# Three PSUM banks in turn for h, gate and up, three for the mixer, and new orders of the steps

## The reference

```python
zxbcdt = u @ W_in                        # 256 -> 512 (z) + 768 (x, B, C) + 8 (dt)
xBC = silu(causal_conv4(xBC) + conv_b)   # four taps along the tokens
dt = softplus(dt + dt_bias);  A = -exp(A_log)
y, _ = ssd(x * dt, A * dt, B, C, 32)     # a state-space scan, 8 heads of 64, state 128
y = (y + x * D) * silu(z)
y = y * rsqrt(mean(y**2) + EPS) * norm_scale
x1 = layernorm(u + y @ W_out)
```

```python
gate, up = x1 @ dequant(Wg).T, x1 @ dequant(Wu).T      # 256 -> 2048 each
out = layernorm(x1 + (gelu(gate) * up) @ dequant(Wd).T) # 2048 -> 256
```

## Time and profile before

| | |
|---|---|
| median of 3 runs | 956.86 us (954.81 to 960.31) |
| profiled execution | 955.87 us, span 954.1 us |
| PE busy | 853.1 us (89%), 5476 products |
| DVE busy | 709.3 us (74%) |
| ACT busy | 546.9 us (57%) |
| GpSimd busy | 70.0 us (7%) |
| mean granted clock of TensorE | 0.962 of full |

### The profile page before, as it was taken

How to read it: one execution, slowest core, us unless ns; L and a number is a source line. 1 busy time by engine, 2 the same in 40 slices (tenths; PEclk the granted TensorE clock), 3 DMA queues, 4 the chain that set the end, 5 groups by cost and what they waited for, 6 DMA issues and landing times.

```text
span 954.1 us, 16326 instructions
## 1 busy us (share of the span) xinstructions
PE 853.1 (89%) x5476; PEld 743.2 (78%) x5476; DVE 709.3 (74%) x1600; ACT 546.9 (57%) x1002; POOL 70.0 (7%) x105
## 2 busy tenths in 40 slices
...
GB/s 135 137 27 62 42 117 106 23 34 73 140 13 23 66 145 55 22 66 113 87 22 44 88 127 6 22 66 146 54 22 67 123 79 13 56 102 1 1 34 12
DMA packets 37578, 61.32 MB, mean 64 GB/s; under 512 B 3264, under 2 KB 25888, under 8 KB 37536
## 3 DMA queue, kind: packets, MB, share of 16 engines
...
q10 hardware_dynamic: 432, 0.03, 0.0%
...
## 4 chain that ended last, share of the span: by engine, by line
PE 61%; DVE 14%; DMA 8%; issue 8%; ACT 5%; POOL 3%; SPq 1%; DVEq 0%; POOLq 0%; ACTq 0%
DMA dec<-spread 5%; PE gate_bank L535 5%; PE mixer L535 5%; PE up_bank L535 5%; PE up_bank L537 5%; PE up_bank L536 4%; PE gate_bank L537 4%; PE gate_bank L536 4%; PE down L535 4%; PE mixer L537 4%; PE down L536 4%; PE down L537 4%; PE mixer L536 4%; PE mixer L602 3%; ACT dec L764 2%
## 5 line engine op out<-in xcount | busy, mean ns | idle before, releaser
L535 PE MATMUL down<-wd_hi,in_hi 128*128 128x256 f32 x512 | 144.4, 282 | 1.0 <-DVE in_lo L1062 1.0
L536 PE MATMUL down<-wd_lo,in_hi 128*128 128x256 f32 x512 | 143.1, 279 | 0.0
L537 PE MATMUL down<-wd_hi,in_lo 128*128 128x256 f32 x512 | 142.8, 279 | 0.0
L535 PE MATMUL gate_bank<-hT_hi,wg_hi 128*128 128x512 f32 (+1 forms) x288 | 113.8, 395 | 23.6 <-ACT act_sb L797 23.6
L931 DVE SCALAR_TENSOR_TENSOR xbc<-mixer,chan,xbc 128x510 f32<-128x510 f32 (+1 forms) x162 | 110.9, 684 | 26.6 <-ACT xbc L732 25.4
L1062 DVE TENSOR_TENSOR in_lo<-act_sb,in_hi 128x512 fp32r<-128x512 f32 (+1 forms) x144 | 90.0, 625 | 51.7 <-ACT in_hi L783 51.0
L783 ACT ACTIVATE in_hi<-act_sb 128x512 fp32r<-128x512 f32 (+1 forms) x144 | 82.7, 574 | 64.3 <-PE down L537 53.0
L1076 DVE SCALAR_TENSOR_TENSOR act_sb<-up_bank,act_sb 128x512 f32<-128x512 f32 (+1 forms) x144 | 90.3, 627 | 37.9 <-PE up_bank L537 19.3
L535 PE MATMUL up_bank<-hT_hi,wu_hi 128*128 128x512 f32 (+1 forms) x288 | 107.7, 374 | 5.6 <-DVE act_sb L1076 5.6
L797 ACT ACTIVATE act_sb<-gate_bank 128x512 f32<-128x512 f32 (+1 forms) x144 | 78.7, 547 | 50.7 <-PE gate_bank L537 50.1
L537 PE MATMUL up_bank<-hT_hi,wu_lo 128*128 128x512 f32 (+1 forms) x288 | 107.3, 373 | 0.0
...
## 6 DMA issues: line engine op xcount, KB each, us to landing
...
```

The costliest lines, as they stand in the source:

```text
L535: nc.tensor.matmul(dst, lh, rh, start=first, stop=False, skip_group_check=True)
L536: nc.tensor.matmul(dst, lh, rl, start=False, stop=False, skip_group_check=True)
L537: return nc.tensor.matmul(dst, ll, rh, start=False, stop=last, skip_group_check=True)
```

## The change

Of the eight banks, three (`ffn0` to `ffn2`) now serve h, gate and up in turn, three the mixer, and two down as before. Gate of unit n goes to a bank that up of unit n-2 had, so it waits for inter of unit n-2; up of unit n goes to the bank that gate of unit n-1 had, so it waits for that gelu. The order of the mixer's steps is new in the first run and in full groups (z products between the x products; A one slot earlier; H and L of a tile together), the last group keeps its lists. Chunks 0 to 12 are now done in the first run and 13 to 23 in the second, one behind each unit, all with take-off and lower; the subtraction on DVE is gone. `dt`'s links, and SP's places for `spread`, `load_uT` and `keep_h`, are new too.

```diff
+MIXER_BANKS = 3
-    "full": ["dt", "x4", "x5", "x0", "z0", "x1", "CB0", "CB1", "z1", "x2", "z2", "A", "x3", "z3", "XT0", "Y0", "XT1",
-             "Y1", "Yoff0", "XT2", "S0", "op0", "Y2", "XT3", "S1", "op1", "Y3", "Yoff1", "S2", "op2", "S3", "op3"],
+    "full": ["dt", "x4", "z0", "x5", "x0", "z1", "x1", "z2", "x2", "x3", "A", "z3", "CB0", "XT0", "CB1", "Y0",
+             "XT1", "S0", "op0", "Y1", "Yoff0", "XT2", "Y2", "XT3", "S1", "Y3", "Yoff1", "op1", "S2", "op2",
+             "S3", "op3"],
...
-    "full": [["x5"], ["x0", "z0"], ["x1", "CB0", "CB1", "z1"], ["x2", "z2"], ["A", "x3", "z3"], ["H0"],
-             ["L0", "XT0", "X0", "W0"], ["Y0", "H1"], ["L1", "XT1", "X1", "W1"], ["Y1", "g0", "H2"],
-             ["L2", "XT2", "X2", "S0", "W2"], ["op0", "g1", "Y2", "H3"], ["L3", "XT3", "X3", "S1", "W3"],
-             ["op1", "g2", "Y3"], ["S2", "op2", "g3"], ["S3", "op3", "ln1"], ["ln2"]],
-    "first": [["x5", "x0", "x1", "z0", "CB0", "A", "x2", "z1", "x3", "z2", "z3", "XT0", "H0", "L0", "H1", "X0", "L1",
-               "W0", "X1", "Y0", "W1", "XT1", "Y1", "g0", "S0", "op0", "g1", "S1", "op1", "ln1", "ln2"], []],
+    "full": [["z0", "x5"], ["x0", "z1"], ["x1", "z2", "x2"], ["x3", "A"], ["z3", "CB0"], ["H0", "L0", "XT0"],
+             ["X0", "W0"], ["CB1", "Y0", "H1", "XT1", "L1"], ["X1", "g0"], ["W1", "S0", "H2", "L2", "op0", "Y1",
+             "X2"], ["XT2", "H3", "W2"], ["L3", "X3", "Y2", "g1"], ["XT3", "W3", "S1"], ["Y3", "op1", "g2"],
+             ["S2", "op2", "g3"], ["S3", "op3", "ln1"], ["ln2"]],
+    "first": [["x5", "x0", "x1", "z0", "A", "z1", "x2", "CB0", "x3", "z2", "H0", "z3", "L0", "XT0", "H1", "X0",
+              "W0", "L1", "X1", "W1", "Y0", "XT1", "Y1", "g0", "S0", "op0", "g1", "S1", "op1", "ln1", "ln2"], []],
...
-BESIDE_FIRST = 12
+BESIDE_FIRST = 13
-VALUE = {FIRST: {"x0": [2], "x1": [3], "x2": [4], "x3": [5], "XT0": [6], "L1": [7], "XT1": [8], "Y1": [9],
+VALUE = {FIRST: {"win": [0, 1], "x5": [2], "x0": [3], "A": [4], "x2": [5], "L0": [6], "XT0": [7], "X1": [8], "g0":
+         [9, 10], "g1": [11], "S1": [12]}, 0: {0: [13], 1: [14], 2: [15], 3: [16], 4: [17], 5: [18], 6:
...
-SPREAD_FIRST, SPREAD_NEXT = 6, 22
+SPREAD_FIRST, NEXT_UT, KEEP_FIRST, SPREAD_NEXT = 6, 14, 15, 20
...
-            return (GB, UB, *OB)[c % 4]
+            return (*FB[0:2], *OB)[c % 4] if c < BESIDE_FIRST else OB[1]
...
+        def gate_up(n):
+            return FB[(2 * n + 2) % 3], FB[2 * n % 3]
...
-                    for wh, wl, b, done, read in ((wg_hi, wg_lo, GB, G_ready, gelu_ok),
-                                                  (wu_hi, wu_lo, UB, U_ready, inter_ok)):
-                        if n:
-                            wait(pe, read, f, n)
+                    gate_b, up_b = gate_up(n)
+                    for wh, wl, b, done in ((wg_hi, wg_lo, gate_b, G_ready), (wu_hi, wu_lo, up_b, U_ready)):
+                        if b is up_b:
+                            if n:
+                                wait(pe, gelu_ok, f, n)
+                        elif n >= 2:
+                            wait(pe, inter_ok, f, n - 1)
+                        elif n == 0 and kind_of(f) != "first":
+                            wait(pe, gelu_ok, f - 1, NF)
...
-            def rest(c):
-                dve.wait_ge(wt_hi.sem, c + 1)
-                dve.wait_ge(wt_lo.sem, c)
-                upper, lower = prep_dst(c)
-                tt(lower, chunk_out(c), f32(upper), ALU.subtract).then_inc(wt_lo.sem, 1)
```

More of the change, by code:

```diff
@@ L91, in stages @@
 def stages(g, units):
-    order, at, slots = [], 0, SLOTS[kind_of(g)]
+    order, at, slots = [], 0, SLOTS["second" if isinstance(g, int) and g == 0 else kind_of(g)]
     for n, slot in enumerate(slots):
@@ L243, in chunk_bank @@
         def chunk_bank(c):
-            return (GB, UB, *OB)[c % 4]
-        MB = [ctx.enter_context(nc.psum_tensor(f"mixer{b}", [P, 512], F32)) for b in range(4)]
-        GB = ctx.enter_context(nc.psum_tensor("gate_bank", [P, 512], F32))
-        UB = ctx.enter_context(nc.psum_tensor("up_bank", [P, 512], F32))
+            return (*FB[0:2], *OB)[c % 4] if c < BESIDE_FIRST else OB[1]
+        MB = [ctx.enter_context(nc.psum_tensor(f"mixer{b}", [P, 512], F32)) for b in range(MIXER_BANKS)]
+        FB = [ctx.enter_context(nc.psum_tensor(f"ffn{b}", [P, 512], F32)) for b in range(3)]
         OB = [ctx.enter_context(nc.psum_tensor(f"down{b}", [P, 512], F32)) for b in range(2)]
-        bank_ready = [sig(f"mixer{b}_ready", len(USES["full"][b::4]), len(USES["first"][b::4])) for b in range(4)]
+        bank_ready = [sig(f"mixer{b}_ready", len(USES["full"][b::MIXER_BANKS]),
+                          len(USES["first"][b::MIXER_BANKS])) for b in range(MIXER_BANKS)]
         small_in = sig("small_in", 0, step=16)
@@ L650, in ffn @@
                     else:
-                        wait(pe, gelu_ok, f - 1, NF)
                         wait(pe, inter_ok, f - 1, NF)
-                    for k, (b, done) in enumerate(((GB, G_ready), (UB, U_ready))):
+                    for k, (b, done) in enumerate(zip(FB, (G_ready, U_ready))):
                         for t in range(tiles(f)):
@@ L677, in prep @@
             def prep(g, item):
-                for c in TAKE_OFF.get(item, ()) if kind_of(g) == "first" else ():
+                for c in TAKE_OFF[g].get(item, ()):
                     b = chunk_bank(c)
@@ L813, in prep @@
                     upper(c)
-                for c in LOWER[g].get(item, ()) if kind_of(g) == "first" else ():
+                for c in LOWER[g].get(item, ()):
                     lower(c)
@@ L819, in any_mixer @@
                 mixer(name, g)
-                if name == "x1" and kind_of(g) == "first":
+                if name == WOUT_AT and kind_of(g) == "first":
                     act.wait_ge(wout_in.sem, 16)
@@ L838, in _ @@
             nc.scalar.activation(win_hi[:, :, X0:B0], x_raw, ACT.Copy).then_inc(win_top.sem, 1)
-            upper(0)
+            prep(FIRST, "win")
             act.wait_ge(z_in.sem, 16)
@@ L845, in _ @@
             mixer("x4", FIRST)
-            upper(1)
+            prep(FIRST, "x4")
             run_all(act, any_mixer, ffn, prep)
@@ L1066, in ffn @@
                 if kind == "F1":
-                    for k, b in enumerate((GB, UB)):
+                    for k, b in enumerate(FB[0:2]):
                         wait(dve, hT_h, f, k + 1)
@@ L1140, in _ @@
             decode(0)
-            value(0)
-            value(1)
             dve.wait_ge(win_top.sem, 1)
```

54 lines of the change are left out of this document (26 added, 28 removed), and 13 rows, old and new, of tables (LINKS, SLOTS, USES).

## The result

The new kernel takes 950.05 us (median of 6 runs, 947.93 to 951.14) against 958.47 us of the kernel before (6 runs, 954.81 to 961.78). The ratio is 0.9909, with a 95% interval of 0.9882 to 0.9936: a gain of 8.4 us, where the forecast was 24. The profiled execution took 951.14 us, with a span of 949.4 us; it is 4.7 us shorter than the profiled one of before. A median in the table of experiments is of all executions of a kernel, while the ratio leaves out slow ones, over 1.5% above the fastest of the same kernel (two of eight for "old order, SP", none elsewhere).

The account below looks back on a forecast made before the run. PE bounds the loop; a chain through DVE, ACT and DMAs decides the first and second runs. Gains of 9 + 6.5 + 5 + 0 + 3.5 = 24 us from 955.9 gave 932 us, range 915 to 951.

Parts of the forecast that it names:

- sign: Whole kernel: faster, meaning below 952 us, chance 0.84; same 0.07; slower, above 962 us, 0.09.
- Second run behind H0: Second run from H0 to F1: DVE about 1 us less, take-offs fit PE's idle time; gain 0, bounds -6 and +5.
- rival 1: The start gives little: second-run take-offs delay PE's units, scales still hold the first run; 942 us, chance 0.18.
- Second run up to H0: Second run, F1 to H0: less DVE work ahead of `spread` brings H0 earlier; gain 5 us, bounds 1 and 8.
- First run: First run to F1: H0 leaves its place behind chunk 6, W0 starts earlier; gain 6.5 us, bounds 0 and 10.
- The loop: Six passes: 1.3 (gelu) + 0.4 (Y0's wait for W0) - 0.2 (Y1) = 1.5 us each; 9 us, range -9 to +10.
- A's earlier place: Loop: A a slot earlier removes H0's 0.62 us wait on ACT and with it PE's 1.3 us a pass.
- Three mixer banks: Loop: three mixer banks in place of four fit by 1.5 us; charge 0, bounds 0 and 3.
- rival 3: Loop slower: three mixer banks too few, products wait for taps and hold PE; 967 us, chance 0.09.
- Last group and end: Last group and end: half of PE's 4.5 + 2.1 us waits for inter and gelu go; 3.5 us, bounds 0 and 6.
- Rival 5: Loop: the clock dips to 0.98 over a pass, costing 2 us a pass; 944 us, chance 0.03.
- Rival 2: The start gives more: behind H0 shrinks by 5, first run by 9, end by 6; 921 us or less, chance 0.15.

Follow-up runs that it names:

- old order, SP: The kernel of 14: the new kernel with the old order in full groups and both SP edits; 961.89 us, ratio 1.0005.
- both SP edits: On the new kernel, `spread` sent behind chunk 17's scales, not 19's, and tile 2's loads put before chunk 22's scales: 938.16 us, ratio 0.9773.
- 15: The kernel before with SPREAD_NEXT 19 in place of 22 and tile 2's loads before chunk 22's scales: 949.63 us, ratio 0.9900.
- 14: The new kernel with the old order in full groups, plus both SP edits: 961.89 us, ratio 1.0005; 64.9 us behind H0.
- 10: experiment 5's kernel with value, upper, take-off and lower of chunks 13 to 23 on an eighth of the columns: 63.2 us behind H0, against 70.1.
- 9: experiment 5's kernel with take-offs and lowers of chunks 13 to 23 on an eighth of the columns: 68.3 us behind H0, against 70.1.
- Experiment 2: The new kernel with SPREAD_NEXT 18 in place of 20, so `spread` follows chunk 17's scales, not 19's: 941.84 us, ratio 0.9838.
- 8: The new kernel with chunk 6's value and chunk 5's upper again ahead of H0 in the first run: 957.41 us, ratio 0.9969.
- experiment 7: The new kernel, in its new order, with the old banks (four for the mixer, one each for gate and up): 957.28 us, ratio 0.9974.
- 6: The new kernel (new banks, first run and chunk places) with the old order in full groups: 975.63 us, ratio 1.0172.
- experiment 1: The new kernel with tile 2's second-run loads before chunk 22's scales, not behind chunk 23's: 943.37 us, ratio 0.9853.
- experiment 5: The new kernel with both SP edits: 938.16 us, ratio 0.9773; second run 117.45 us.
- experiment 3: The new kernel with low parts of chunks 13 to 23 subtracted on DVE again, without second-run take-offs and lowers: 950.58 us, ratio 0.9918.
- experiment 12: The new kernel with both SP edits and the low parts of chunks 13 to 23 subtracted on DVE: 936.27 us, ratio 0.9769.

## Why the prediction was off

Its sign and its range held (950.05 is inside 915 to 951, at the edge); its size was three times the one measured. That the time stayed inside the range is luck: by the two profiled executions the first run gave 6.2 us more than its term, the second run 18.5 less, and the loop and the end 7.1 less. By its own steps:

- **"Second run behind H0: I take 0, bounds -6 and +5": this step failed.** It was -14.6. Of that 6.1 us are ACT's wait for tile 2's `dec` ahead of H2. The prediction counted PE's, DVE's and ACT's work behind H0, and of SP only what stood ahead of `spread`. It didn't look at the four loads of scales between tile 1's loads and tile 2's. They tie tile 2 to the value of chunk 21, and the change moved that value from unit 6 to unit 8. With both SP edits 8.4 us are left. The runs don't split them cleanly. The kernel before with the same edits takes 65.2 us behind H0 too, so that like with like it is 5.0 us (15), and these come with the new order (14) at a clock that was not the same. Thin chunk work takes 6.9 us off the same stretch (10), so order and chunk work act together; the take-offs, which the prediction's rival 1 feared for PE, are worth 1.8 at a lower clock (9).
- **"Second run up to H0: gain 5 us": it was 1.1.** The working took DVE to be the chain and counted the 7 us of work that left it; DVE's busy time fell by just that (39.42 to 32.45 us). But what `spread` waited for wasn't the amount of DVE's work: it was the value of chunk 17, which DVE does behind unit 4, 7 us after the rows were ready. In the kernel before it waited for that of chunk 19, done behind unit 4 as well. The place on SP moved by two chunks, its place among the units by none, and `spread` went out 46.0 us behind F1 in place of 47.4. Experiment 2 gives 7.4 us back by that number alone. The range of 1 to 8 for this term just held it.
- **First run, 6.5 us: it was 12.7**, above the bound of 10. Its mechanism held (8), and W0 alone came 10.4 us earlier; the term was mis-sized, and behind W0 another 2.3 us went.
- **The loop, 1.5 us a pass: 1.1.** The wait of 1.3 us is gone and ACT idles 4.1 us ahead of H3 at no cost, as forecast; the 0.4 at Y0 didn't go but became 0.7, and Y1, for which I charged 0.2, waits for nothing. The prediction credited A's earlier place first and the banks "besides". A's place took H0's wait away, but no time off a pass (102.7 to 103.2 us in experiment 7); it needed the banks as well. "Three mixer banks: 0" held only for the new order. In the old one this was rival 3: passes of 105.4 to 105.9 us at a clock of 1.00, some 2.5 to 3 us over those of before, and 107.4 to 111.1 in the first three, at 0.93 to 0.98 (6).
- **Last group and end, 3.5 us: -1.1.** The working took half of PE's waits for gelu and inter as won. They did go, but PE then waited for CB0's input and for W0 instead, 7.9 us in all against 7.8. In the last group nothing was won (90.35 us with the old banks in experiment 7, 90.24 with the new ones in experiment 1, both at 1.00); at the end 1.4 us came back (45.6 us before, 44.2 now). The loss itself goes with the clock: the last group took 90.2 us at 1.00 in experiment 1 and 93.8 at 0.96 in the new kernel.
- **Rival 5, the clock:** from the second pass on it is 1.00 with three banks in turn, as with one. The trace doesn't agree here with what the Trainium skill's page "TensorE: Matmul & The Clock Gate", section "A second HAM failure mode: psum-queue depth-cycling", says of a PE that idles briefly at each turn of its banks. In the old order with the new banks the second pass of experiment 6, with waits of 2.5 and 1.9 us, was at 0.97, but in experiment 14 every pass from the second on was at 1.00, the fourth with waits of 2.5 and 2.1 us; so the waits alone don't decide it.
- **Sums.** Rival 2's parts are 5 + 2.5 + 2.5 = 10 us, not 11, which makes it 922. The loop's lower bound of -9 counts the 3 us of the banks and leaves out the bounds of 1.5 at W1 and 2 at H3.

## What to carry to other kernels

Where one queue carries two kinds of transfers in a fixed order, read each transfer's start as "which wait of an earlier entry let it go", and follow that wait to the place in the program to which it is tied; moving work on the compute engines moves that place too. A number that moves an entry two places in such a queue may move it by nothing in time. Before an engine's saved work is counted as a gain, look whether the thing at the end of its chain was ready before it was sent. And where an edit repairs the new kernel, try it on the old one too: what it gives there belongs to neither the change nor its repair.

## What the runs showed of the chip

The same products of the last group (554 or 555 in the profile) took 90 to 94 us, the longer the lower the granted clock. Stretch rows of experiments 1 and 5:

```profile
806.17:896.41 90.24, 84.44 (x555) 75.09 (x553) 58.89 (x142) 46.51 (x85) 5.42 (x8) 1.00 0.13 42
```

```profile
797.43:891.05 93.62, 87.61 (x554) 77.69 (x553) 58.92 (x142) 46.50 (x85) 5.43 (x8) 0.96 0.12 41
```

DVE and ACT are as busy in both; PE is 3.2 us longer at a mean of 0.96, a mixture of the 2.4 GHz and the 1.2 GHz level. The first loop pass, behind a second run in which PE is about three quarters busy, took 100.9 us at 0.98 in one kernel (2) and 105.8 us at 0.94 in another (8), with the same instructions. So a difference of 3 to 5 us between two single executions of these kernels can be the clock's. The stretches of the second run, by which the experiments are judged, aren't free of it: behind H0 they ran at 0.76 to 0.92.

Behind H0, where PE isn't full, taking its take-offs away went with a lower clock each time: 0.76 in experiment 3 against the new kernel's 0.86, and 0.81 in experiment 9 and 0.78 in experiment 12 against 0.88 in experiment 5. The products left on PE then took longer, so such a test can show less than the work was worth.
